# Expert stages of a six-stage kernel: seven unrolled chunks of mixed width against an engine loop over chunks of five batches

## The reference

```python
logits = layernorm(x) @ router_w + router_b                 # 8 experts
top, idx = lax.top_k(logits, 2); probs = softmax(top)
pos = place of each (choice, token) among those of its expert   # cumulative count
cap = int(1.2 * 2 * 256 // 8)                                  # 76 rows per expert and batch
einp[idx, pos] += x_row                                        # rows over cap are dropped
h, g = einp @ w_fc + b_fc, einp @ w_gate + b_gate              # 128 -> 512, per expert
o = silu(h * g) @ w_proj + b_proj                              # 512 -> 128
out = sum over the 2 choices of probs * o[idx, min(pos, cap - 1)]
x = x + 0.5 * out
```

## Time and profile before

| | us |
|---|---|
| median of 3 runs (lowest, highest) | 2738.7 (2730.96, 2742.22) |
| the profiled execution, its own time | 2738.68 |
| its span (first to last instruction) | 2736.9 |
| TensorE busy, of the span | 2259.9 (83%) |
| VectorE busy | 1361.3 (50%) |
| ScalarE busy | 1283.6 (47%) |
| GpSimd busy | 593.3 (22%) |
| mean granted TensorE clock | 0.907 |

### The profile page before, as it was taken

The page is one execution under the profiler, slowest core; times in us unless marked ns, Lnnn a source line. Parts: engine busy times, 40 slices in busy tenths (PEclk is TensorE's granted clock), DMA queues, the critical chain, the costliest instruction groups (busy, mean ns, idle before and its releaser), DMA issues.

```text
span 2736.9 us, 44615 instructions
## 1 busy us (share of the span) xinstructions
PE 2259.9 (83%) x13878; PEld 1743.4 (64%) x13878; DVE 1361.3 (50%) x4152; ACT 1283.6 (47%) x2551; POOL 593.3 (22%) x687
## 2 busy tenths in 40 slices
PE   4979989667597789739999999999976668679974
PEld 3979979566354456536777777777765545345654
DVE  5867767543242334435555655556553324243443
ACT  3755557533232344426666666666643324234432
POOL 2112210133523433240000000000003351542234
PEclk9999999778797899969999999999996889789987
DMA  6070000011111122110000000000001111212222
GB/s 222 0 265 27 0 0 0 8 39 44 49 51 51 55 60 61 51 37 1 0 0 0 0 0 0 0 0 0 0 2 30 41 53 46 68 51 68 72 55 73
DMA packets 123488, 108.01 MB, mean 39 GB/s; under 512 B 14524, under 2 KB 103092, under 8 KB 123008
## 3 DMA queue, kind: packets, MB, share of 16 engines
q1 hardware_dynamic: 105952, 77.05, 9.0%
q0 software_dynamic: 16384, 27.68, 4.0%
q10 hardware_dynamic: 1056, 2.10, 0.3%
HBM read 51.86 MB, written 60.82 MB: 41 GB/s over the span
## 4 chain that ended last, share of the span: by engine, by line
PE 42%; another core or an unknown queue 4%; issue 4%; DVE 2%; ACT 2%; POOL 0%; DMA 0%; ACTq 0%; POOLq 0%; DVEq 0%; SPq 0%
PE moe_bank L1517 5%; PE lin_bank L982 4%; PE moe_bank L1531 4%; PE moe_bank L1521 4%; PE lin_bank L902 4%; PE lin_bank L910 4%; PE lin_bank L929 4%; PE lin_bank L921 4%; PE lin_bank L958 3%; PE lin_bank L974 2%; PE lin_bank L945 1%; PE moe_bank L1507 1%; DVE moe_act L1683 0%; DVE all_x L1701 0%
## 5 line engine op out<-in xcount | busy, mean ns | idle before, releaser
L1587 ACT ACTIVATE moe_fc<-moe_bank,all_b_fc 128x512 f32<-128x512 f32 (+3 forms) x448 | 244.6, 549 | 679.8 <-PE moe_bank L1517 330.9
L1517 PE MATMUL moe_bank<-moe_rowsT,all_w_fc 128*128 128x512 f32 (+3 forms) x896 | 386.0, 515 | 152.4 <-ACT moe_fc L1587 73.7
L1683 DVE SCALAR_TENSOR_TENSOR moe_act<-moe_bank,all_b_moe_gate,moe_fc 128x512 f32<-128x512 f32 (+3 forms) x448 | 255.9, 577 | 430.3 <-PE moe_bank L1521 207.4
L1521 PE MATMUL moe_bank<-moe_rowsT,all_w_gate 128*128 128x512 f32 (+3 forms) x896 | 372.9, 500 | 24.1 <-issue 18.0
L1435 POOL DMA_INDIRECT rows_in<-moe_xn,moe_put_at x256 | 250.0, 977 | 580.6 <-DVE moe_put_at L1671 506.3
L1445 POOL DMA_INDIRECT moe_landed<-rows_out,moe_take_at x256 | 256.1, 1000 | 481.7 <-issue 269.1
L1517 PEld LDWEIGHTS moe_bank<-moe_rowsT,all_w_fc 128*128 128x128 f32 x896 | 165.4, 213 | 242.1 <-issue 101.2
L1531 PE MATMUL moe_bank<-all_w_proj,moe_act 128*128 128x128 f32 x2432 | 305.2, 282 | 16.9 <-issue 15.8
L1531 PEld LDWEIGHTS moe_bank<-all_w_proj,moe_act 128*128 128x128 f32 x2432 | 294.4, 199 | 17.0 <-issue 15.7
L1521 PEld LDWEIGHTS moe_bank<-moe_rowsT,all_w_gate 128*128 128x128 f32 x896 | 175.8, 212 | 164.2 <-issue 122.8
L1692 DVE TENSOR_TENSOR moe_expert_out<-moe_bank,all_b_proj 128x512 f32<-128x512 f32 (+3 forms) x112 | 58.1, 519 | 388.0 <-remote 230.9
(11 more groups left out here) (214 smaller groups left out, 3749.0 us busy)
## 6 DMA issues: line engine op xcount, KB each, us to landing
moe_rows<-rows_in SPq DMA_DIRECT2D x48, 256.0 KB
rows_out<-moe_expert_out SPq DMA_DIRECT2D x48, 256.0 KB
rows_in<-all_zeros SPq DMA_DIRECT2D x1, 9728.0 KB, 28.1
rows_out<-all_zeros SPq DMA_DIRECT2D x1, 9728.0 KB, 53.2
rows_in<-moe_xn,moe_put_at POOLq DMA_INDIRECT x256
moe_landed<-rows_out,moe_take_at POOLq DMA_INDIRECT x256
moe_rows<-rows_in SPq DMA_DIRECT2D x16, 192.0 KB
rows_out<-moe_expert_out SPq DMA_DIRECT2D x16, 192.0 KB
```

The source lines that it names most:

```text
L1517: nc.tensor.matmul(bank[FC + j % 2][:, 0:c.width], k.w_fc[:, e, j * P:(j + 1) * P], rowsT[:, i % 2, 0:c.width], start=True, stop=True).the ...
L1521: nc.tensor.matmul(bank[GATE + j % 2][:, 0:c.width], k.w_gate[:, e, j * P:(j + 1) * P], rowsT[:, i % 2, 0:c.width], start=True, stop=True) ...
L1587: nc.scalar.activation(fc[:, j, 0:c.width], bank[FC + j % 2][:, 0:c.width], ACT.Identity, bias=k.b_fc[:, e * MC + j:e * MC + j + 1]).then_ ...
L1683: nc.vector.scalar_tensor_tensor(act_in[:, i % 2, j, 0:c.width], bank[GATE + j % 2][:, 0:c.width], k.b_moe_gate[:, e * MC + j:e * MC + j + ...
```

## The change

`moe_stage` is rewritten; the setup stage only writes a longer table of batch row numbers. In words:

- The rows are cut at batch borders. Six chunks of five batches (380 rows, computed as 384) and a last one of two batches (152 rows). There are still 7 x 8 units.
- Chunks 1 to 5 are the body of an engine loop on all five engines (`Fori(1, LAST)`); chunks 0 and 6 are written out. Waits in the body compare with register numbers; `nop`s stand between some waits and the instructions behind them.
- Routing is done batch by batch to the end: `choose_masks`, `count` and `assign` run once per batch, each in a slot of its own, with single buffers (before: `xT` and `logits` double, the rest per chunk). While chunk c is computed, batches 5c+6 to 5c+10 are routed. Before the first chunk batches 0 to 5 are routed, and five of them must be scattered before the first load.
- GpSimd scatters and gathers batch by batch, in turn.
- The gather tables of a chunk are copied first (`take_tables`, two VectorE copies per chunk), `combine` waits also for that copy.
- Rows and expert outputs have four buffers (before two), loads run three units ahead (before two).

```diff
-CHUNKS = (128, 256, 512, 512, 512, 384, 128)
-ROUTE_IN = {0: ((1, 0, 2), (2, 14, 2)), **{c: ((c + 2, 2, 3),) for c in range(1, len(CHUNKS) - 2)}}
-COMBINE_IN = {1: (29, 1), 2: (14, 2), 3: (12, 2), 4: (12, 2), 5: (7, 3), 6: (17, 8)}
+SET, PHASES, LAST_SET = 5, 7, 2
+BLOCKS = 3
+WIDE, LAST_WIDTH = BLOCKS * P, LAST_SET * CAP
+ROUTE_SLOTS = (2, 6, 11, 16, 23)
+ROUTE_LAGS = (("norm", 0), ("transpose", 2), ("router", 3), ("choose", 4), ("mask", 5), ("count", 7), ("assign", 8))
+COMBINE_SLOTS = (12, 17, 21, 26, 30)
+LAST_COMBINES = (20, 27)
+POOL_ORDER = (("scatter", 0), ("kept", 0), ("gather", 0), ("scatter", 1), ("gather", 1), ("scatter", 2), ("gather", 2),
+              ("scatter", 3), ("gather", 3), ("scatter", 4), ("gather", 4))
...
             @block.gpsimd
...
-                for n in range(3):
-                    scatter(n)
-                for c in plan:
-                    rows_kept(c)
-                    for b in c.done:
-                        gather(b)
-                    if c.n + 3 < len(plan):
-                        scatter(c.n + 3)
+                for j in range(2 * SET):
+                    scatter(0, j)
+                with pool.Fori(1, LAST) as c:
+                    phase(c)
+                rows_kept(LAST)
+                for j in range(SET):
+                    gather(LAST, j)
+                rows_kept(LAST, before=0)
+                for j in range(LAST_SET):
+                    gather(LAST, j, before=0)
...
             @block.tensor
...
+                for i in range(-1, SET):
+                    transpose_x(-1, i)
+                    if i >= 0:
+                        count(-1, i - 1)
+                    router(-1, i)
+                count(-1, SET - 1)
+                transpose_rows(0, 0)
+                phase(0)
+                with pe.Fori(1, LAST) as c:
+                    phase(c)
+                phase(LAST, routing=False)
+                down(LAST, EXPERTS - 1)
...
             @block.vector
...
+                def phase(c, routing=True, combines=COMBINE_SLOTS):
+                    if not (isinstance(c, int) and c == 0):
+                        take_tables(c)
+                    for s in range(SLOTS_PER):
+                        e = s // MC
+                        multiply(c, e, s % MC)
+                        if routing:
+                            for what, i in route_at.get(s, ()):
+                                if what == "norm":
+                                    normalise(c, i)
+                                if what == "choose":
+                                    choose(c, i)
+                                if what == "mask":
+                                    choose_masks(c, i)
+                                if what == "assign":
+                                    assign(c, i)
+                        if s in combines:
+                            combine(c, combines.index(s))
+                        if s % MC == MC - 1 and (e or not (isinstance(c, int) and c == 0)):
+                            bias_out(c, e - 1)
```

More of the change, by code:

```diff
@@ L1410, in _, with hold_wait @@
[L1410 to L1420 removed]
+                def hold_wait():
+                    sp.nop(nofuse=True)
@@ new lines, in phase @@
+                def phase(c):
+                    for i in range(EXPERTS):
+                        if i + 3 < EXPERTS or not (isinstance(c, int) and c == LAST):
+                            load(c, i + 3)
+                        if i or not (isinstance(c, int) and c == 0):
+                            keep(c, i - 1)
+                    if out is not None and not (isinstance(c, int) and c in (0, LAST)):
+                        store(c, 1)
+                sp.wait_ge(k.zeroed, 32)
+                for i in range(3):
+                    load(0, i)
@@ new lines, in rows_kept, with phase @@
+                def rows_kept(c, before=1):
+                    for i in range(DEEP):
+                        pool.wait_ge(kept[i], moved_rows(c, EXPERTS - DEEP + i) - before * PER_BUFFER)
+                        hold_wait()
+                    pool.wait_ge(taken.sem, taken.at(c, lag=-before))
+                    hold_wait()
+                def phase(c, scatters=True):
+                    order = POOL_ORDER if scatters else [w for w in POOL_ORDER if w[0] == "gather"]
+                    for what, j in order:
+                        if what == "scatter":
+                            scatter(c, SET + j)
+                        if what == "kept":
+                            rows_kept(c)
+                        if what == "gather":
+                            gather(c, j)
@@ L1524, in down, with count @@
-                def down(i):
-                    c, e = unit(i)
-                    pe.wait_ge(act_sb, 2 * i + 2)
-                    if i:
-                        pe.wait_ge(down_sb, i)
-                    for j in range(c.blocks):
+                    last.then_inc(logits_ps.sem, 1)
+                def count(c, i):
+                    pe.wait_ge(mask_sb.sem, mask_sb.at(c, j=item(i)))
+                    if not (isinstance(c, int) and c < 0 and i < 0):
+                        pe.wait_ge(routed.sem, routed.at(c, j=item(i) - 1))
+                    for t in range(TILES):
+                        ps = bank[COUNT][:, t * TKE:(t + 1) * TKE]
+                        second = bank[COUNT][:, t * TKE + EXPERTS:(t + 1) * TKE]
+                        nc.tensor.matmul(ps, k.tri[:, :], mask[:, t, :, :].rearrange("p k e -> p (k e)"), start=True, stop=False)
+                        if t:
+                            nc.tensor.matmul(ps, k.ones[:, :], mask[:, t - 1, :, :].rearrange("p k e -> p (k e)"), start=False, stop=False)
+                        for s in range(TILES):
+                            last = nc.tensor.matmul(second, k.ones[:, :], mask[:, s, 0, :], start=False, stop=(s == TILES - 1))
+                    last.then_inc(count_ps.sem, 1)
@@ L1625, in normalise, with link @@
[L1625 to L1643 removed]
+                def link(ins, c, i, n):
+                    ins.then_inc(chain.sem, 1)
+                    dve.wait_ge(chain.sem, chain.at(c, j=item(i) * LINKS + n))
@@ new lines, in _ @@
+                normalise(-1, -1)
+                for i in range(-1, SET):
+                    if i + 1 < SET:
+                        normalise(-1, i + 1)
+                    choose(-1, i)
+                    choose_masks(-1, i)
+                    assign(-1, i)
+                phase(0, combines=[])
+                with dve.Fori(1, LAST) as c:
+                    phase(c)
+                phase(LAST, routing=False, combines=LAST_COMBINES)
+                bias_out(LAST, EXPERTS - 1)
+                for j in range(len(LAST_COMBINES), SET):
+                    combine(LAST, j)
@@ L1739, in moe_stage @@
+                dve.wait_ge(combined.sem, combined.at(LAST, j=-1))
+                take_tables(LAST, before=0)
+                for j in range(LAST_SET):
+                    combine(LAST, j, before=0)
+                dve.wait_ge(combined.sem, combined.at(LAST, j=LAST_SET - 1))
+                nc.vector.memset(k.flag[:, :], 0.0).then_inc(taken.sem, 1)
+                dve.wait_ge(taken.sem, taken.at(LAST, j=2))
         k.leave(outer)
```

675 lines of the change are left out of this document (318 added, 357 removed).

## The result

The changed kernel takes 2670.66 us (2667.81 to 2673.28, four runs) beside 2740.02 us for the kernel before: ratio 0.9753, 95% interval 0.9728 to 0.9778. That is 69 us less, where 123 were forecast; the measured time lies inside the range of 2540 to 2765.

The account below looks back on a forecast made before the run. Long unbroken runs of indirect DMAs delaying TensorE were taken as the bound. 72 + 5 x (72 + 12 + 4) + 52 + 21 + 9 = 594, plus 18 start = 612 against 673.6 us per stage; both stages save 123: 2616 us, range 2540 to 2765.

Parts of the forecast that it names:

- five loop chunks: Chunks 1 to 5 of an expert stage: 5 x (72 us computing and routing, 12 pairs, 4 VectorE).
- The price of a pair: GpSimd's scatter and gather groups meeting as eight indirect DMAs: 3 us each, ends 1.3 and 6.5, 12 us per loop chunk.
- Routing and VectorE: Per loop chunk: batch routing on TensorE 6 us; VectorE's small work, mostly covered by TensorE, 4 us, bounds 0 and 10.
- The loop itself: 0: Register waits and edges of the engine loop cost 0 apart from VectorE's 4 us, as in the linear attention.
- The rival of code loading: VectorE's loop code is fetched again at ten loop edges, 10 us each: +100 us, 2716 us; chance 0.12.
- Start, chunk 0, last chunk: Per expert stage: start +18 us from 20 scatters before the load, chunk 0 72 us, last chunk 52 us.
- The end: From the last output bias to the stage's end: 21.1 us before and after, two batches to gather in both.
- SyncE: 0: Loads wait for their chunk's five scatters, four output buffers cover waiting stores: 0; if GpSimd is late, loads are late next.
- The rival of the number of DMAs: Idle time follows the number of indirect DMAs, not run length: 29.7 us per loop chunk, +177, 2793 us; chance 0.15.
- the signs named: Profile after: clock over 0.9, output bias waits well under 60 us, few units 10 to 14, none above 25; wrong: chunks above 98.
- a short run hardly costs: Long unbroken runs of indirect DMAs on GpSimd delay TensorE's work, 0.74 us per DMA in 28; short ones hardly do.

Follow-up runs that it names:

- few_gathers: The changed kernel with three of a batch's four gathers left out, the one left feeding all four additions: 2423.5 us, ratio 0.8849 to the kernel before.
- ahead: The changed kernel with a short pause (128x8 write) behind each group of four and each gather one place earlier: 2460.8 us, ratio 1.0408 to the kernel before.
- before_rested: The kernel before with a pause (128x512 write and wait) behind each batch's four scatters and four gathers: 2399.3 us, ratio 0.8758 to the kernel before.
- set 3: Third set of four follow-up kernels, on chip 2, sharing runs of the kernel before, which took 2365.2 us there.
- set 1: First set of four follow-up kernels, on chip 2, sharing runs of the kernel before, which took 2741.0 us there.
- sets 1 and 2: First two sets of four follow-up kernels each, on chips 2 and 11; the kernel before took 2741.0 us and 2738.6 us there.

## Why the forecast was right in direction and wrong in size

Second stage, forecast and measured:

| term | forecast | measured |
|---|---|---|
| start, more than before | 18 | 34.0 - 13.8 = 20.2 |
| first unit and chunk 0 | 9 + 72 | 2128.6 - 2049.2 = 79.4 |
| five loop chunks | 440 | 2585.2 - 2128.6 = 456.6 |
| last chunk | 52 | 54.8 |
| end | 21 | 25.6 |
| gain against 673.6 | 61.6 | 37.0 |

The first stage gave the other 32 us; its five loop chunks took 471.6 us.

The mechanism held, and one size in it did not. *The price of a pair* is the term that was mis-sized: 3 us in the forecast, 4.8 us or somewhat more measured (93.0 - 73.9, over four pairs), so 19 us a chunk instead of 12. I had it from two stretches of eight that cost little and one row of sixteen, and those two stretches were cheap ones: unit by unit against few_gathers the third unit, which two pairs touch, costs 6.6 us more, the fifth 3.4, the sixth 6.3. 6.5 was the upper bound given.

*Routing and VectorE* were taken too high together: 6 + 4 us on 65.4, measured at most 73.9 - 65.4 = 8.5, since some of the delay is left in that chunk. So part of the miss on the pairs was made good by luck: a first loop chunk of 93.0 us stands against 88. VectorE is busy half the time and is not a bound.

*The loop itself: 0* was wrong for one stage. The nearest row was a loop whose code stays held. The rival of code loading has its mechanism in the first stage alone and was four times too large: five passes cost 18.1 and 4.4 us where they could be measured alone, not 50 and 50. Both bodies come from the same function and differ in little but their place in the program; that the place decides is not shown.

*Start, chunk 0, last chunk* came within 3 us each. The last chunk's run of 20 costs 17.6 us (54.8 - 37.2). *The end* was 4.5 us off.

*SyncE: 0* held in the changed kernel. In ahead it became the next thing late, as the forecast said it would if GpSimd is late.

*The rival of the number of DMAs* is refuted by before_rested: 72 DMAs in 111 us cost next to nothing once there is a pause behind each four. Of the signs named, three held: the granted clock is 0.91 where over 0.9 was named, no unit is above 25 us, and chunks stayed below 98 us. Two did not: the waits of the output bias were to be well under 60 us and are 68.7, and the long units were to be a few at 10 to 14 us, where two of a chunk's eight take 16 to 20 in most chunks. Both say the same as the price of a pair.

*What I did not see* is the larger part. The reading "a short run hardly costs" led me to value the order of the groups. The rows would also have borne the cheaper test, a pause and nothing else, which gives 339 us where the change gives 69. By an estimate across sets, which takes the stages of set 3, short pauses included, as free of the delay, the stage of before loses about 176 us to it (673.6 - 497.7) and that of the changed kernel about 103 (616.4 - 513.7, with the order of ahead). The change would then save 73 of these a stage and pay 36 for itself: 20 at the start, 16 in the stage. Where the effect is absent only the price would be left. That was measured on ahead (4.1% slower), not on the changed kernel itself.

**What stays open.** Why a run of indirect DMAs holds back TensorE and its signals, and whether other engines' signals come late in it too; why not in set 3, whose results name the same chip number as those of set 1 half an hour earlier, with indirect DMAs of the same length (0.98 to 1.01 us); and 65 of the 91 us that unrolling gave, which the loop's own 26 us do not explain. The Trainium skill, "SBUF — State Buffer", section "SBUF: two separate sides", has DMAs and TensorE not contend there. Set 3 agrees with it, with no such wait beside the same DMAs, and nothing in sets 1 and 2 shows that the delay arises in that memory. What else ran on the machine in any set is not on record.

## What to carry to other kernels

Where GpSimd issues more than four indirect DMAs in a row and TensorE's consumers show long waits with an impossible or remote releaser, first put a pause of 1.3 to 1.5 us behind each four (a small write and a wait for it). With 1.3 us it gave 12% where it was needed; a pause of 0.9 us cost 0.7% where it was not. Reorder or restructure only against that baseline. Price a new loop by whether its body is loaded again at each pass, and an effect of unknown cause by runs on more than one chip and at more than one time before building on it.

## What was unexpected of the hardware

- A pause of 1.3 us on GpSimd behind four indirect DMAs removes nearly all of TensorE's delay (110.25 of 111.1 us busy). With 1.5 us the output bias of the changed kernel still waits 7.6 us for nothing that this core shows, with 1.0 to 1.1 us 26.4, with the 0.3 us between any two DMAs 68.7.
- The program alone does not bring the delay about: the same kernel takes 2740 us in two sets and 2365 in a third, each within 0.5%.
- In a long run TensorE starts products that wait for nothing the profile shows one at a time, eight records in 10.5 us.
- An eight costs 4.8 us on average in the changed kernel and almost nothing in some places, a run of 20 costs 14 to 18.
- Instructions are loaded anew at each pass of a loop in one stage (five packets; the loop costs 3.6 us a pass) and not in the other, with a body from the same function.
